# Attention algebra of a fused layer in a basis of 255 features and a constant, chain one iteration shorter

## The reference

```python
x = L0_attn_x                              # (4, 2048, 256) f32
xn = _layernorm(x)                         # over the 256 features
# attention, per batch (C = 2048 tokens, L = 256 features)
Q = xn @ Wq.T + bq;  K = xn @ Wk.T + bk;  V = xn @ Wv.T + bv
Q, K = Q / |Q|, K / |K|                    # norms over the 2048 tokens
tailor_sum = 1.0 / (L + einsum('bnc,bc->bn', Q, sum(K, -1) + 1e-6))
matrix = einsum('bmn,bcn->bmc', K, V)
matrix_sum = value_sum + einsum('bnm,bmc->bcn', Q, matrix)
s = xn + gamma * matrix_sum * tailor_sum
# feed-forward, 256 -> 704 -> 256, x and h quantized in blocks of 16
h = silu(fp4_linear(xn, w_gate)) * fp4_linear(xn, w_up)
g = silu(fp4_linear(h, w_down))
return x + s * g
```

## Times and profile before

| | us |
|---|---|
| median of 3 runs | 663.29 (663.21 to 665.48) |
| the profiled execution | 665.72 |
| its span | 663.9 |
| PE busy / DVE busy / ACT busy / POOL busy | 585.5 / 583.3 / 422.5 / 289.4 |
| setup up to the end of iteration 0 | 60.1 |
| iterations 1 to 4 | 59.2 |
| iterations 5 to 11 (chain of batch 0) | 120.9 |
| iterations 12 to 19 and 20 to 27 (batches 1 and 2) | 146.1 and 148.6 |
| iterations 28 to 31 (batch 3) | 73.1 |
| tail, behind DVE's last L855 | 55.9 |

### The profile page before, as it was taken

One profiled execution on the slowest core, in us unless ns is written; L12 is line 12 of the kernel. 1 busy time (PEld: TensorE's weight loads), 2 busy tenths in 40 slices (PEclk: granted clock), 3 DMA queues, 4 the chain that ended last, 5 costly groups with the idle time before them and its releaser, 6 DMA issues.

```text
span 663.9 us, 15805 instructions
## 1 busy us (share of the span) xinstructions
PE 585.5 (88%) x5139; PEld 449.3 (68%) x5139; DVE 583.3 (88%) x1257; ACT 422.5 (64%) x1052; POOL 289.4 (44%) x224
## 2 busy tenths in 40 slices
PE   0567799999999899999998889999998899998767
PEld 0444577777777677778786667778786677776656
DVE  7968999889989999999999989989999998777644
ACT  3575888767777787666677667666676775543210
POOL 5253455333643455535635435435634432225116
PEclk9997999999999999999999989999998999997799
DMA  7010000000000011011111111011111011310023
GB/s 241 16 33 17 17 18 17 17 17 17 17 17 33 33 30 64 8 49 49 49 50 49 50 48 52 2 49 49 50 49 49 33 34 34 98 46 33 33 79 127
DMA packets 17762, 29.43 MB, mean 44 GB/s; under 512 B 2704, under 2 KB 5136, under 8 KB 17680
## 3 DMA queue, kind: packets, MB, share of 16 engines
q1 hardware_dynamic: 17680, 28.39, 13.0%
HBM read 19.99 MB, written 8.39 MB: 43 GB/s over the span
## 4 chain that ended last, share of the span: by engine, by line
PE 39%; DVE 33%; issue 16%; ACT 5%; POOL 4%; DVEq 1%; DMA 1%; POOLq 0%; SPq 0%; ACTq 0%
PE GU L1377 16%; DVE hg L888 5%; PE DS L1387 5%; PE G L1441 4%; DVE hq L896 3%; DVE ham L855 3%; DVE xq L837 3%; DVE h L848 3%; PE DS L1389 3%; PE TR L1339 2%; PE G L1460 2%; POOL ht L530 2%; PE GU L1397 2%; ACT sil L599 2%; DVE y L907 1%
## 5 line engine op out<-in xcount | busy, mean ns | idle before, releaser
L1377 PE MATMUL GU<-wgu,xqT 128*128 128x352 f16 x1536 | 256.0, 318 | 3.4 <-DVE y L907 2.1
L1377 PEld LDWEIGHTS GU<-wgu,xqT 128*128 128x128 f16 x1536 | 148.8, 100 | 79.3 <-issue 2.9
L599 ACT ACTIVATE sil<-GU,wkap 128x352 f32<-128x352 f32 x128 | 70.9, 554 | 84.3 <-PE GU L1377 81.3
L530 POOL TENSOR_TENSOR ht<-h,hrr 128x1408 f32<-128x1408 f32 x32 | 82.8, 2588 | 68.1 <-DVE hrr L862 68.1
L848 DVE SCALAR_TENSOR_TENSOR h<-GU,wkap,sil 128x352 f32<-128x352 f32 x128 | 70.6, 552 | 30.7 <-ACT sil L599 27.1
L1387 PE MATMUL DS<-wdT,hqT 128*128 128x256 f16 x704 | 89.6, 277 | 1.3 <-ACT hqT L606 1.3
L488 POOL TENSOR_TENSOR xnat<-xs,xnat 128x512 f16<-128x512 f32 (+1 forms) x32 | 37.0, 1158 | 110.8 <-DVE ht L885 106.8
L1387 PEld LDWEIGHTS DS<-wdT,hqT 128*128 128x128 f16 x704 | 67.9, 100 | 11.3 <-ACT hqT L606 1.4
L495 POOL TENSOR_TENSOR xt<-xs,xrr 128x512 f32<-128x512 f32 x32 | 34.0, 1062 | 94.4 <-DVE hq L896 85.5
L642 ACT ACTIVATE gring<-DS,hun 128x256 f32<-128x256 f32 (+1 forms) x64 | 30.2, 472 | 54.4 <-issue 34.1
L543 POOL TENSOR_TENSOR o<-y,xe 128x512 f32<-128x512 f32 x25 | 36.0, 1438 | 65.0 <-DVE y L907 36.6
(11 more groups left out here) (173 smaller groups left out, 1095.2 us busy)
## 6 DMA issues: line engine op xcount, KB each, us to landing
xin<-in_L_attn_x SPq DMA_DIRECT2D x34, 256.0 KB, 2.8
xe<-in_L_attn_x SPq DMA_DIRECT2D x25, 256.0 KB, 2.9
out<-o SPq DMA_DIRECT2D x25, 256.0 KB, 2.1
algebra<-in_L_ffn_w_down SPq DMA_DIRECT2D x1, 704.0 KB, 6.4
gring<-in_L_ffn_w_gate SPq DMA_DIRECT2D x1, 640.0 KB, 4.4
gring<-in_L_ffn_w_up SPq DMA_DIRECT2D x1, 640.0 KB, 5.1
xs<-in_L_attn_x SPq DMA_DIRECT2D x2, 256.0 KB, 4.0
xt<-in_L_attn_x SPq DMA_DIRECT2D x2, 256.0 KB, 4.6
```

What stands on the lines that cost most here:

```text
L530: g.tensor_tensor(paired(ht[:, 0:2 * I]), paired(h[:, q]), spread(hrr[:, q], 4 * CB), ALU.mult).then_inc(S["ht_d"], 1)
L599: a.activation(sil[:, c], GU[:, c, 0, 0:CH], ACT.Silu, scale=wkap[:, 0:1]).then_inc(S["sil_d"], 1)
L1377: last = t.matmul(GU[:, c, m, 0:CH], xqT[:, k, j, 2 * a_ + kc], wgu[:, b_, kc, 2 * m + c], start=(z == 0 and kc == 0), stop=(z == 2 and kc ...
```

## The change

The tokens of a normalized row add up to zero over the 256 features, so feature 255 is minus the sum of the others. The new kernel writes a constant (1, in the kernel's scale 256) in its place, and subtracts each weight row's column 255 from its other columns; the bias goes into column 255. The Gram matrix then holds the column sums and the token count, and every bias lies inside the products. Gone are the steps sums, cols and row, the rank-one terms of t1q, t1k and raw, the lift matmul of every s, the accumulator outputs of ACT, and norm_products on POOL. t1q and raw are now copied out by ACT (a new table COPIES), and DVE makes the squares for the norms (squares_q; squares_k with an accumulator output). A step own_basis (DVE, in iteration 1) builds the weights; the transposes of the attention weights move from the setup to iterations 2 and 3. LAGE becomes 10, and the steps lie closer.

```diff
-TRING = 14
-GRING = 10
+TRING = 13
+GRING = 9
-LEADA, LEADB, LEADN, LEADT, LAGH, LAGE = 3, 2, 2, 1, 2, PB + 3
+LEADA, LEADB, LEADN, LEADT, LAGH, LAGE = 3, 2, 2, 1, 2, PB + 2
+FIRST = LAGE - PB + 3
...
+        ASKS = {(-3, 0, 2): "weights_q", (-3, 1, 2): "weights_k", (-2, 0, 2): "weights_v",
+                (-1, 1, 2): "gram0_first", (0, 0, 1): "gram0_last", (0, 1, 2): "gram1", (1, 0, 2): "turn", (1, 1, 2): "t1q",
...
-                g.tensor_tensor(slot[:, :, D:2 * D], xs[:, q], slot[:, :, 0:D], ALU.subtract).then_inc(S["xlo"], 1)
+                g.tensor_tensor(slot[:, :, D:2 * D - 1], xs[:, q, :, 0:D - 1], slot[:, :, 0:D - 1], ALU.subtract).then_inc(S["xlo"], 1)
...
-            def norm_products(b):
-
-                for z, (t1, wT) in enumerate(((t1q, wqT), (t1k, wkT))):
-                    wait(pool, "t1_ev", 2 * b + 2)
-                    g.tensor_tensor(prod[:, z], t1[:, :, :], wT[:, :, :], ALU.mult).then_inc(S["prod1"], 1)
-                    wait(pool, "prod1", 2 * b + z + 1)
-                    g.tensor_tensor(prod[:, z, 0], prod[:, z, 0], prod[:, z, 1], ALU.add).then_inc(S["prod_d"], 1)
...
+            def copy(b, step):
...
+                if step == "t1q":
+                    wait(act, "tq_mm", b + 1)
+                    a.copy(t1q[:, :, :], matrices).then_inc(S["tq_ev"], 1)
+                if step == "raw":
+                    wait(act, "inv_d", b + 1)
+                    wait(act, "raw_mm", b + 1)
+                    for m in range(KD):
+                        last = a.activation(raw[:, m], matrices[:, m], ACT.Copy, scale=inv[:, 2 + m:3 + m])
...
-            def xn_out(u, at, j, done):
...
-                for m in range(KD):
-                    last = a.activation(rows_[:, :, m], from_[:, :, m], ACT.Copy, accum_out=xsum[:, m, at + j:at + j + 1])
-                last.then_inc(S[done], 1)
...
+            def xn_out(u, j, done):
...
+                a.copy(ring(xnT, u, TRING)[:, j], TR[:, j, 512:1024].rearrange("p (z t) -> p z t", t=P)).then_inc(S[done], 1)
...
+                slot = ring(xnat, u, RING)
+                if isinstance(u, int) and u < RING:
+
+                    act.wait_ge(S["xone_d"], 2)
+                    a.copy(slot.rearrange("p j (z d) -> p j z d", z=2)[:, :, :, D - 1:D], xone[:, :, :, :])
...
-                if step == "sums":
-                    wait(dve, "x_ev", 2 * ((b + 1) * PB - 1))
-                    v.tensor_reduce(ssum[:, :], xsum[:, :, :], AX.X, ALU.add).then_inc(S["sum_rd"], 1)
...
-                if step in ("t1q", "t1k"):
...
+                if step == "squares_q":
+                    wait(dve, "tq_ev", b + 1)
+                    v.tensor_tensor(prod[:, :, :], t1q[:, :, :], wqT[:, :, :], ALU.mult).then_inc(S["prod_d"], 1)
+                if step == "squares_k":
+
+                    wait(dve, "tk_mm", b + 1)
                     for m in range(KD):
+                        last = v.scalar_tensor_tensor(kprod[:, m], G[:, m * D:(m + 1) * D], 1.0, wqkv[:, 1, m], ALU.mult, ALU.mult,
+                                                      accum_out=nrm[:, 2 + m:3 + m])
+                    last.then_inc(S["tk_d"], 1)
...
+                if step == "own_basis":
...
+                    v.tensor_tensor(every[:, :, 0:D - 1], every[:, :, 0:D - 1],
+                                    every[:, :, D - 1:D].broadcast_to([P, 3 * KD, D - 1]), ALU.subtract).then_inc(S["w_sub"], 1)
...
-            v.tensor_scalar(bcolc[:, :], bcol[:, :], float(TOKENS), None, ALU.mult).then_inc(S["bpre"], 1)
-            v.tensor_scalar(cbq[:, :], bbc[0:1, 0], float(TOKENS), None, ALU.mult).then_inc(S["bpre"], 1)
...
-                t.matmul(bank, lift[:, :], Rx[:, columns], start=False, stop=True).then_inc(S["s_d"], inc)
...
                 if step == "raw":
-                    wait(pe, "nrm2", b + 1)
+                    wait(pe, "nrm_d", b + 1)
                     for m in range(KD):
                         for k in range(KD):
-                            t.matmul(G[:, m * D:(m + 1) * D], wkT[:, k, m * P:(m + 1) * P], t1q[:, k], start=(k == 0), stop=False)
-                        last = t.matmul(G[:, m * D:(m + 1) * D], bbc[0:1, 1, m * P:(m + 1) * P], tqrow[:, :], start=False, stop=True)
+                            last = t.matmul(G[:, m * D:(m + 1) * D], wkT[:, k, m * P:(m + 1) * P], t1q[:, k],
+                                            start=(k == 0), stop=(k == KD - 1))
```

More of the change, by code:

```diff
@@ L162, in build @@
         HLs, As, Gs, raw = (algebra[:, z] for z in range(4))
[L163 to L168 removed]
+        t1q, prod, kprod = HLs, wqkv[:, 0], raw
         nrm = sb("nrm", [P, 4])
         inv = sb("inv", [P, 4])
[L171 to L172 removed]
         den = sb("den", [P, 2])
@@ L260, in spread_in_order @@
             return ap.rearrange("p (n e o) -> p n e o", o=1, e=2).broadcast_to([P, blks // 2, 2, BLK])
-        ASKS = {(-1, 1, 2): "gram0_first", (0, 0, 1): "gram0_last", (0, 1, 2): "gram1", (1, 0, 2): "cols",
-                (1, 1, 1): "turn", (2, 0, 1): "t1q", (2, 1, 0): "t1k", (3, 0, 2): "norms", (3, 1, 2): "raw",
-                (4, 0, 2): "tailor", (4, 1, 2): "product", (5, 0, 2): "top", (5, 1, 2): "high_low", (6, 0, 1): "row"}
-        ANSWERS = {(0, 1, 0): "gram0", (1, 0, 0): "sums", (1, 0, 1): "gram1", (1, 1, 0): "cols", (1, 1, 2): "turn",
-                   (2, 0, 2): "t1q", (2, 1, 1): "t1k", (3, 1, 0): "norms", (4, 0, 1): "raw", (4, 1, 0): "tailor",
-                   (5, 0, 1): "product", (5, 1, 0): "top", (6, 0, 0): "high_low", (6, 0, 1): "row"}
@@ new lines, in build @@
+        ANSWERS = {(-4, 1, 1): "own_basis", (0, 1, 0): "gram0", (1, 0, 1): "gram1", (1, 1, 0): "turn", (2, 0, 1): "squares_q",
+                   (2, 0, 2): "squares_k", (2, 1, 1): "norms", (3, 1, 0): "tailor", (4, 0, 1): "product", (4, 1, 1): "top",
+                   (5, 0, 1): "high_low"}
+        COPIES = {(-3, 1, 0): "weights_q", (-2, 0, 0): "weights_k", (-2, 1, 0): "weights_v", (2, 0, 0): "t1q", (3, 0, 1): "raw"}
+        ASKS_END = {(-1, 1, 2): "gram0_first", (0, 0, 0): "gram0_last", (0, 1, 0): "gram1", (1, 0, 0): "turn", (1, 0, 2): "t1q",
+                    (1, 1, 1): "t1k", (2, 0, 0): "norms", (2, 0, 2): "raw", (2, 1, 1): "tailor", (3, 0, 0): "product",
+                    (3, 0, 2): "top", (3, 1, 1): "high_low"}
@@ L280, in at_step @@
+        ANSWERS_END = {(0, 0, 2): "gram0", (0, 1, 2): "gram1", (1, 0, 1): "turn", (1, 1, 1): "squares_q", (1, 1, 2): "squares_k",
+                       (2, 0, 1): "norms", (2, 1, 2): "tailor", (3, 0, 1): "product", (3, 1, 0): "top", (4, 1, 2): "high_low"}
+        COPIES_END = {(1, 1, 0): "t1q", (2, 1, 0): "raw"}
         def at_step(table, table_end, b, at):
@@ L961, in answer @@
[L961 to L968 removed]
+                    wait(dve, "tk_d", b + 1)
@@ L1481, in ask @@
+                if step == "norms":
+                    wait(pe, "tk_d", b + 1)
+                    wait(pe, "prod_d", b + 1)
+                    for n in range(KD):
+                        for k in range(KD):
+                            last = t.matmul(G[:, n:n + 1], prod[:, k, n * P:(n + 1) * P], ones32[:, 0:1],
+                                            start=(k == 0), stop=(k == KD - 1))
                     last.then_inc(S["norm_mm"], 1)
                 if step == "raw":
-                    wait(pe, "nrm2", b + 1)
+                    wait(pe, "nrm_d", b + 1)
```

299 lines of the change are left out of this document (116 added, 183 removed).

## The result

The changed kernel takes 638.59 us (median of 4 runs, 637.63 to 638.81); the one before took 664.15 beside it (4 runs, those of the table and one more). The ratio is 0.961, 95% interval 0.959 to 0.963. It is 25.6 faster by the medians; the forecast was 36 (627.3). The time lies inside the range of 617 to 642, at its slow end, 2.4 from the rival "the waits come back" (641). The profiled execution took 638.52, its span 636.7: 27.2 less than the span before. I compare that with the terms.

What follows compares the result with a forecast made beforehand. In the loop DVE's own work plus waits pushed in by PE's attention bursts bound it, in the tail a chain of waits. Terms 3.2 - 0.7 - 7 - 8 - 8 - 4.5 - 11 = -36.0 off median 663.3 give 627.3; range 617 to 642.

Steps and rivals of the forecast that it cites:

- the waits come back: First of the rivals: in the tighter chain each batch keeps its 4.9 of waits, DVE over 3 at i=3; 641, chance 0.15.
- The tail: Stretch after the last batch: earlier product, no row pass and cheaper uses of Mx make it 11 us shorter (10 to 12).
- own_basis: New DVE step in iteration 1: adds 3.2 us in all, its subtraction at most 2.0.
- Batch 0: First batch: 7 us shorter, from 5 - 1.1 of DVE work, 4 of waits, and 2 against it.
- setup: Start of the kernel: PE's wait for cbq shrinks by 0.6, ACT's copies by 0.3; 0.7 us gained.
- batch 3: Last batch, bound by PE: PE's work nearly the same, its waits shrink; 4.5 us shorter.
- DVE's work in a batch: Instructions and a stall removed, squares added: 5 us less per batch, bounds 4.4 and 6.
- PE's busy time of a batch: cols, part of raw and the lift matmuls go: PE loses 6.6 of batch 1's 137.1.
- Waits in all 4.9 now, 1.9 then: 3 us: DVE's waits in batches 1 and 2: 3 us less each, with 5 of DVE work 8 us shorter each.
- my fourth rival: Emptier PE falls to half clock in i=5, 6 and -1, 16 places of 2.5: 667, slower; chance 0.03.
- The second rival: squares_q stands behind POOL's ht, up to 2.5 a batch: 637, chance 0.08; its sign is squares_q over 1 us.
- The lift: Matmul gone from every half of s: 0.3 us of PE an iteration, 0.7 less wait behind gram, 1.7 in the tail.

Runs made afterwards that it cites:

- experiment 1: The changed kernel with the ask high_low moved behind the first gate_up group of i=5, in the last batch behind the down product: 630.34 us, ratio 0.946.
- 9: The kernel before the change with iterations 12 to 27 written out instead of a machine loop: 658.82 us, ratio 0.990.
- 7: The changed kernel with high_low asked later, half of the next batch's gram0 a step ahead and no machine loop: 617.67 us, ratio 0.929.
- experiment 2: The changed kernel with 48 unread transposes keeping PE busy while it waits for kap in i=4 of batches 0 to 2: 635.11 us, ratio 0.952.
- 10: The changed kernel with iterations 12 to 27 written out instead of a machine loop, nothing else moved: 623.32 us, ratio 0.935.
- Experiment 4: The changed kernel with a seventh matmul of 128 columns put back in every half of s: 640.75 us, ratio 0.961.

## Why the prediction was right, and where it was not

**The steps that held.** The tail's Mx is used 27.8 behind the last reduction of ham (28 in the forecast, had 37.8), and its products are 0.66 apart:

```profile
604.24 1.12 PE L1453 MATMUL G<-id,mt 128*128 128x128 f32 x4 [3.81 <-DVE kap L971]
...
621.64 2.56 PE L1342 MATMUL GU<-Mx,xnT 128*128 128x256 f16 x22 [2.38 <-DVE Mx L979]
...
631.72 0.48 DVE L908 SCALAR_TENSOR_TENSOR y<-GU,unm,gring 128x256 f32<-128x256 f32 x1 [0.17 <-PE GU L1342]
632.38 0.48 DVE L908 SCALAR_TENSOR_TENSOR y<-GU,unm,gring 128x256 f32<-128x256 f32 x1 [0.17 <-PE GU L1342]
```

The tail gave 13.0 (forecast 11) though it holds the same mistake as the loop: PE stood 3.81 at high_low, and moving that ask gave 3.1 more. The 2 us above the forecast are largely luck of the clock: before, the first six products with Mx took 1.44 at a granted clock of 0.50, now the first 22 take 2.56 at 1.00. In experiment 1 Mx is there 4.7 earlier, but the clock is at 0.57 in four us of that row, and so the tail shows only 3.1. own_basis is one run of DVE from 73.20 to 76.44: 3.2, of which the subtraction took 1.74. Batch 0, setup and batch 3 came out at 6.6, 0.7 and 5.7. The sum for batch 0, "5 + 4 - 2 = 7", leaves out the 1.1 named just before it; with it the forecast was 5.9, and its parts measure 3.1 of DVE's busy time and 3.5 of its idle time. In batch 3 PE is busy 66.2 of 67.4 (68.2 of 73.1 before), so there, as forecast, PE's waits went. DVE's work in a batch fell by 4.2 where I had 5; without the machine loop by 5.0. PE's busy time of a batch was to fall by 6.6: between batch 2 of 9 and of 7, both at full clock, it falls by 6.1; with the loop only by 3.9 and 3.3, as the half clock stretches what is left.

**The step that failed** is the one on the waits of batches 1 and 2, "Waits in all 4.9 now, 1.9 then: 3 us"; 6.2 were measured. Its parts:

- The chain's last wait was not in my list at all. I had looked only at DVE's waits for silus, and of PE's I weighed those behind cols, turn, raw and norms. In the trace before, PE also waits for mtop, kap and Mx. I asked of each ask that moved which burst it makes, but not of high_low whether its input is there. In the new table its ask is one place behind the answer to top in the tables, but PE runs ahead of DVE, and DVE has hg, two hq, an h and a y ahead of that answer, 3.3 from 337.09. Price: 2.9 and 3.0 in the iteration behind it (experiment 1; batch 2 as a whole gained 1.8), and of DVE's wait of 2.8 the clock is 2.4 (experiment 2). This is my fourth rival in small, "one or two more such places cost 2.5 to 5". I gave it 0.03 as a case that turns the sign; as a part of the forecast it belonged in the sum.
- The wait behind gram1 stayed at 1.55 (0.7 forecast): the same burst of 3.6 showed more, probably as DVE had less to do ahead of it (argued; no run shows it). The wait at i=3 was 1.6 (1 forecast), the first rival's, at its place and less than its "over 3". These two made 1.5 a batch; with the 2.8 of high_low that is the 4.3 by which the waits of batch 1 were missed, and with 0.8 of DVE's work about the 5.0 of its term.
- The jump of the loop made iteration 20 1.9 longer than before; nothing in my working stood for it. It is a part of the 6.8 by which batch 2 missed its term. The whole loop costs the new kernel 12.3 to 15.3, the old one 5.7 to 7.6 (experiments 9 and 10, by spans and by medians).

That the total stayed inside its range is in part luck: without the 3.0 that the other terms gave above forecast, 2.0 of them in the tail, it would be 641.6, at the edge of 642. It lies near the first rival's 641, but not by that mechanism: batches 0 and 3 gave their terms, and the wait at i=3 is the smaller part.

**The sizes inside the DVE term.** squares_q took 1.04 in batches 1 and 2 instead of 0.67 (1.30 in batch 0, 0.68 in batch 3), squares_k 0.84 as forecast and its accumulator reads 0.08 each. The timeline of DVE at squares_q, batch 1, after:

```profile
291.54 1.04 DVE L928 TENSOR_TENSOR wqkv<-algebra,wqT 128x512 f32<-128x512 f32 x1
...
293.54 0.42 DVE L933 SCALAR_TENSOR_TENSOR algebra<-G,wqkv 128x256 f32<-128x256 f32 x1 [0.21 <-PE G L1411]
293.89 0.08 DVE L933 DVE_READ_ACCUMULATOR algebra<-G,wqkv 128x1 f32 x1
```

and POOL's ht, which began ahead of it:

```profile
289.44 2.59 POOL L514 TENSOR_TENSOR ht<-h,hrr 128x1408 f32<-128x1408 f32 x1 [1.45 <-DVE hrr L851]
```

It ends at 292.03 and squares_q 0.55 later: it stood behind the last 0.5 of ht. "On my reading ht ends just before squares_q's turn" was wrong by 0.5. The second rival's sign, "squares_q over 1 us", showed, but its mechanism cost 0.4 a batch, not 2.5. The rule "SBUF: two separate sides" of the page "SBUF — State Buffer" of the Trainium skill, that the two exclude each other for a whole instruction, agrees with it. The rule on instructions with two float32 sources in SBUF, of the page "Vector Engine (DVE) Microarchitecture Reference" of the Trainium skill, "Points that are easy to get wrong", if it is read as half the pace of an instruction with one such source, does not fit this trace: ht on DVE reads two, 1408 elements in 1.61, and the reduction ham reads one, 1408 elements in the same 1.61. Neither has an accumulator output; no run here has one beside two sources in SBUF.

**The lift** went from every half of s. I let it count for 0.7 in batch waits and 1.7 in the tail. Experiment 4 shows 1.6 for the row of sixteen in the tail and nothing in batches 1 and 2.

## What to carry to other kernels

When asks and answers are packed closer, check for each ask of the engine that runs ahead whether its input is already there, not only how long its burst is: such a wait costs the idle time once, and the low clock behind it again, on the engine that was full. Put an ask that waits for a late answer behind a group that can run without it; one place in each of two tables was worth 8 us here. And price a machine loop for itself, by writing it out once: by the spans this change is worth 31.9 without it and 27.2 with it. When two profiles differ in a stretch that the edit does not touch, read the granted clock there before looking for a cause.
